# One attention layer with routed experts: slots of two head pairs, r made once, position copies on ScalarE

## The reference, cut to what matters

```
Q, K, V = X @ Wq + bq, X @ Wk, X @ Wv          # 16 heads of 64
R       = X @ Wr + br                          # 16 heads of 10
extra   = einsum('bhtn,ntp->bhtp', R, D)       # D[n, t, p] = b_nd[n, t - p] where 0 <= t - p < 128, else 0
logits  = Q K^T / 8 + bias + extra             # bias = -1e9 outside that window
out     = softmax(logits) V, then @ Wproj + bproj
# experts: each token goes to 2 of 8 (w1, exact gelu, w2), weighted by a softmax over the two
```

## Time and profile before

| what | value |
|---|---|
| median of three runs | 1502.11 us |
| the profiled execution, its own time | 1502.1 us |
| its span | 1500.3 us |
| TensorE matmul busy | 1390.5 us (93%) |
| VectorE busy | 994.2 us (66%) |
| ScalarE busy | 963.8 us (64%) |
| GpSimd busy | 758.2 us (51%) |
| mean granted TensorE clock | 0.967 of full speed |

### The profile page before, as it was taken

How to read it: one execution, slowest core, us unless ns; L and a number is a source line. 1 busy time by engine, 2 the same in 40 slices (tenths; PEclk the granted TensorE clock), 3 DMA queues, 4 the chain that set the end, 5 groups by cost and what they waited for, 6 DMA issues and landing times.

```text
span 1500.3 us, 37780 instructions
## 1 busy us (share of the span) xinstructions
PE 1390.5 (93%) x10823; PEld 1144.7 (76%) x10823; DVE 994.2 (66%) x4355; ACT 963.8 (64%) x2992; POOL 758.2 (51%) x1520
## 2 busy tenths in 40 slices
PE   2572999999999999999999999799999999999997
PEld 1231788888888888878999999688888888888886
DVE  4677677777777777772222221288888888888886
ACT  1121777777777777775454545387777777777775
POOL 1241566676776667660000000167777666777764
PEclk8695999999999999999999999899999999999999
DMA  9775666666666666645666666567676666767662
GB/s 284 269 247 176 188 177 194 183 180 186 187 189 183 185 190 183 183 128 180 210 192 212 200 204 200 150 189 193 184 193 188 180 185 172 194 186 192 188 177 66
DMA packets 441412, 283.00 MB, mean 189 GB/s; under 512 B 18666, under 2 KB 415508, under 8 KB 441236
## 3 DMA queue, kind: packets, MB, share of 16 engines
q1 hardware_dynamic: 433044, 264.12, 61.1%
q0 software_dynamic: 8192, 16.79, 3.9%
HBM read 135.01 MB, written 145.77 MB: 187 GB/s over the span
## 4 chain that ended last, share of the span: by engine, by line
PE 86%; DVE 5%; SPq 3%; DMA 2%; issue 2%; POOL 1%; ACT 1%; DVEq 0%; ACTq 0%; POOLq 0%
PE ps L1420 14%; PE ps L1440 12%; PE ps L1345 9%; PE ps L1309 9%; PE ps L1310 9%; PE ps L1311 9%; PE ps L1450 9%; PE ps L1409 8%; PE ps L1380 4%; PE ps L1327 1%; DMA skew<-gst 1%; SPq L400 1%; DMA wproj<-in_L_attn_Wproj_dram 1%; DMA xn_d<-xn 1%; SPq L453 1%
## 5 line engine op out<-in xcount | busy, mean ns | idle before, releaser
L810 ACT ACTIVATE prob<-logit,low 128x128 f32<-128x128 f32 x1024 | 403.6, 395 | 232.1 <-DVE low L1120 230.0
L1120 DVE CUSTOM_DVE_ANT_0 logit<-ps,extra 128x128 f32<-128x128 f32 x1024 | 256.4, 288 | 190.8 <-PE ps L1420 179.8
L676 POOL TENSOR_SCALAR prob<-prob,inv 128x128 f32<-128x128 f32 x512 | 189.0, 369 | 237.1 <-DVE inv L1106 233.4
L1420 PE MATMUL ps<-qk 64*128 64x256 f32 (+1 forms) x2048 | 237.7, 351 | 2.2 <-DVE low L1120 2.2
L1420 PEld LDWEIGHTS ps<-qk 64*128 64x128 f32 x2048 | 177.4, 187 | 78.7 <-issue 33.7
L1094 DVE TENSOR_TENSOR probT<-ps,keep 128x256 f32<-128x256 f32 x512 | 214.0, 418 | 26.6 <-PE ps L1409 25.7
L1409 PE MATMUL ps<-ident,prob 128*128 128x128 f32 x1024 | 200.5, 279 | 0.4 <-POOL prob L678 0.3
L1440 PE MATMUL ps<-probT,val 128*64 128x256 f32 (+1 forms) x2048 | 194.7, 332 | 5.4 <-DVE probT L1095 5.4
L810 ACT ACTIVATION_READ_ACCUMULATOR prob<-logit,low 128x1 f32 x1024 | 191.1, 187 | 0.0
L651 POOL CAST r_hi<-r_raw 120x512 fp32r<-120x512 f32 x64 | 39.6, 618 | 297.5 <-ACT r_raw L773 297.4
L678 POOL TENSOR_SCALAR prob<-prob,inv 128x128 f32<-128x128 f32 x512 | 186.9, 365 | 0.0
(11 more groups left out here) (179 smaller groups left out, 2792.2 us busy)
## 6 DMA issues: line engine op xcount, KB each, us to landing
skew<-gst SPq DMA_DIRECT2D x384, 256.0 KB
extra<-skew SPq DMA_DIRECT2D x256, 256.0 KB, 3.4
w1b<-w_d SPq DMA_DIRECT2D x39, 514.0 KB, 3.5
w2b<-w_d SPq DMA_DIRECT2D x39, 320.0 KB, 3.3
x_place<-zero SPq DMA_DIRECT2D x39, 256.0 KB, 2.8
placed<-x_place SPq DMA_DIRECT2D x39, 256.0 KB, 3.7
y_place<-yrow SPq DMA_DIRECT2D x39, 256.0 KB, 2.2
w_d<-w1s SPq DMA_DIRECT2D x1, 4112.0 KB, 11.9
```

Of the source, the lines that this page charges most:

```text
L676: nc.gpsimd.tensor_scalar(prob[:, h, 0:P], prob[:, h, 0:P], inv[:, h, 0:1], 1.0, ALU.mult, ALU.mult).then_inc(norm_made, 1)
L810: ins = nc.scalar.activation(prob[:, h % PB, a:b], logit[:, h % LB, a:b], ACT.Exp, scale=-1.0, bias=low[:, h % LB, t:t + 1], accum_out=tot ...
L1120: ins = nc.vector.tensor_tensor_reduce(out=logit[:, h % LB, a:b], in0=ps[:, S_BANK[n], a:b], in1=extra[:, h, a:b], scale=1.0, scalar=BIG, ...
L1420: mm = nc.tensor.matmul(ps[:, S_BANK[n], cols], qk[rows, pair % 2, 0, q], qk[rows, pair % 2, 1, k], start=True, stop=True)
```

## The change

It regroups attention into double slots d = 0 to 3 of two pairs (four heads) and changes four things.

- TensorE makes the logits of both pairs in one go (banks 0 to 3), then the values, and the outputs later in the same double slot, between keys and a position unit. The transposes of a pair (four) come together and use one bank. The units have one bank instead of two.
- r is made once, in one unit of six products with 80 rows, for all 16 heads. GpSimd rounds it to r_hi and subtracts to r_lo; six DMAs of SyncE (`spread_weights`) then put high, high and low part into rT, which is there twice (even and odd sequences).
- All g are copied by ScalarE.
- VectorE takes one reciprocal for four heads, at the head of the next double slot, and masks the transposes of a pair in two instructions instead of four. The row moves of GpSimd have other places, yget has two buffers, and rows are added in four steps.

The table of units and the start:

```diff
-        UNITS = [(0, 0, "v", 0, 0, 0), (0, 1, "g", 3, 0, 0), (1, 0, "r", 0, 0, 1), (1, 1, "g", 3, 1, 0),
...
+        UNITS = [(0, 0, "v", 0, 0, 0), (0, 1, "g", 2, 1, 0), (0, 2, "r", 0, 0, 1), (0, 3, "g", 3, 0, 0),
...
-        START = [("r", 0, 0), ("r", 1, 0)] + [("g", g, t) for g in range(3) for t in range(2)]
+        START = [(kind, k, t) for _, _, kind, k, t, ahead in UNITS if ahead]
```

The order on TensorE:

```diff
+            def sequence(i, start, heads=True, more=True):
+                for d in range(QUADS if heads else LAG):
...
+                    if to_come:
+                        keys(*later)
                     if heads:
-                        units(i, par, j, 0, more)
-                        logits(i, j)
...
+                        units(i, d, 0, more)
+                        logits(i, d)
+                    if here(i, d - 2, heads, start):
+                        values(i, d - 2)
                     if heads:
-                        units(i, par, j, 1, more)
...
+                        units(i, d, 1, more)
+                    if here(i, d - 1, heads, start):
+                        turn_probs(i, 2 * (d - 1))
+                    if to_come:
+                        keys(later[0], later[1] + 1)
+                    if heads:
+                        units(i, d, 2, more)
+                    if here(i, d - 2, heads, start):
+                        outputs(i, d - 2)
+                    if heads:
+                        units(i, d, 3, more)
+                    if here(i, d - 1, heads, start):
+                        turn_probs(i, 2 * (d - 1) + 1)
```

The way of r:

```diff
+            def spread_weights(seq):
+
+                par = seq % 2
+                sp.wait_ge(r_low, seq + 1)
+                for t in range(2):
+                    wait_from(sp, g_made[t], 4 * (seq - 1))
+                for s, part in enumerate((r_hi, r_hi, r_lo)):
+                    for a in range(2):
+                        sp.dma_start(rT[s * PER * NB:(s + 1) * PER * NB, par, :, a, :].bitcast(F32),
+                                     part[a * PER * NB:(a + 1) * PER * NB, :].bitcast(F32).rearrange("p (k q) -> p k q", q=T)
+                                     ).then_inc(r_in[par], 16)
...
-            def round_weights(seq, k):
-
-                wait_apart(pool, r_copied, 2 * seq + (k + 1), const_made)
-                nc.gpsimd.tensor_copy(r_hi[:, k, :], r_raw[:, k, :]).then_inc(r_high, 1)
+            def round_weights(seq):
+
+                pool.wait_ge(r_copied, seq + 1)
+                if seq > 0:
+                    pool.wait_ge(r_in[(seq - 1) % 2], (seq + 1) // 2 * 96)
+                nc.gpsimd.tensor_copy(r_hi[:, :], r_raw[:, :]).then_inc(r_high, 1)
+                pool.wait_ge(r_high, seq + 1)
+                nc.gpsimd.tensor_tensor(r_lo[:, :], r_raw[:, :], r_hi[:, :].bitcast(F32), ALU.subtract).then_inc(r_low, 1)
...
-                nc.vector.scalar_tensor_tensor(out=rT[:, k, :], in0=r_hi[:, k, :].bitcast(F32), scalar=minus_low[0:RS, :],
-                                               in1=r_raw[:, k, :], op0=ALU.mult, op1=ALU.add).then_inc(r_made, 1)
```

The reciprocals and ScalarE's order:

```diff
+            def inverses(i, quad):
+
+                h = 4 * quad % PB
+                dve.wait_ge(prob_made, i * PAIRS + 2 * quad + 2)
+                wait_from(dve, norm_made, 8 * (i * QUADS + quad - 1))
+                nc.vector.reciprocal(inv[:, h:h + 4, :], total[:, h:h + 4, :]).then_inc(inv_made, 1)
...
+                    units(d, 0)
+                    if to_come:
+                        keys(*later)
                     if heads:
...
+                        exponentials(i, 2 * d, 0)
+                    if here(i, d - 2, heads, start):
+                        heads_out(i, d - 2)
+                    units(d, 1)
+                    if heads:
+                        exponentials(i, 2 * d, 1)
+                    units(d, 2)
+                    if to_come:
+                        keys(later[0], later[1] + 1)
+                    units(d, 3)
+                    if heads:
+                        exponentials(i, 2 * d + 1, 0)
+                        exponentials(i, 2 * d + 1, 1)
```

More of the change, by code:

```diff
@@ new lines, in moves_of, with norms @@
+            def moves_of(i, way, d, more):
+                moves = MOVES_FINAL if way is FORTH and not more else MOVES
+                return [n for n, at_d in enumerate(moves) if at_d == d]
+            def norms(i, d, n):
+                pair = 2 * d + n
+                for h in (2 * pair % PB, 2 * pair % PB + 1):
+                    nc.gpsimd.tensor_scalar(prob[:, h, 0:P], prob[:, h, 0:P], inv[:, h, 0:1], 1.0,
+                                            ALU.mult, ALU.mult).then_inc(norm_made, 1)
+                    nc.gpsimd.tensor_scalar(prob[:, h, P:], prob[:, h, P:], inv[:, h, 1:2], 1.0,
+                                            ALU.mult, ALU.mult).then_inc(norm_made, 1)
@@ L703, in _ @@
+                    if d == 0 and heads and more:
+                        round_weights(i + 1)
             FORTH, BACK = "forth", "back"
@@ L709, in _ @@
                 split_q(s0, 0)
-                for k in range(2):
-                    round_weights(s0, k)
+                round_weights(s0)
                 if way is FORTH:
@@ new lines, in exponentials @@
+            def exponentials(i, pair, t):
+                cols = slice(t * P, (t + 1) * P)
+                act.wait_ge(logit0_made if t == 0 else logit_made, i * PAIRS + pair + 1)
+                if t == 0:
+                    wait_from(act, pT_psum, i * PAIRS + pair + 1 - PB // 2)
+                for h in (2 * pair, 2 * pair + 1):
+                    ins = nc.scalar.activation(prob[:, h % PB, cols], logit[:, h % LB, cols], ACT.Exp,
+                                               scale=-1.0, bias=low[:, h % LB, t:t + 1],
+                                               accum_out=total[:, h % PB, t:t + 1])
+                if t == 1:
+                    ins.then_inc(prob_made, 1)
@@ new lines, in heads_out, with units @@
+            def heads_out(i, quad):
+                act.wait_ge(head_psum, i * QUADS + (quad + 1))
+                wait_from(act, out_psum, i * QUADS + quad)
+                nc.scalar.copy(headT[:, :, :].rearrange("p n t -> p (n t)"),
+                               ps[:, HEAD_BANK, :]).then_inc(head_made, 1)
+            def sequence(i, start, heads=True, more=True):
+                def units(d, place):
+                    for n, kind, k, t, ahead in units_at(d, place, more) if heads else []:
+                        unit(len(START) + i * len(UNITS) + n, kind, k, t, i + ahead)
+                for d in range(QUADS if heads else LAG):
+                    to_come = heads and (d + 1 < QUADS or more)
+                    later = (i, 2 * (d + 1)) if d + 1 < QUADS else (i + 1, 0)
+                    units(d, 0)
+                    if to_come:
+                        keys(*later)
+                    if heads:
+                        exponentials(i, 2 * d, 0)
[11 more added lines that the diff above has]
+                        exponentials(i, 2 * d + 1, 1)
@@ L1137, in sequence @@
-                    for n, kind, k, t, ahead in units_at(j, 0, more) if heads else []:
-                        if kind == "r":
-                            weights(i + 1, k)
-                    if j in ADDS and start == HALF and here(i, -1, heads, start) and heads:
-                        add_rows(i - HALF - 1, ADDS.index(j), i - 1)
+                        copy_probs(i, 2 * (d - 1))
+                    if heads:
+                        bias_sums(i, 2 * d + 1)
+                    if here(i, d - 1, heads, start):
+                        copy_probs(i, 2 * (d - 1) + 1)
@@ L1381, in unit, with units @@
+                        mm = product(ps[0:RP, MISC_BANK, k * T:(k + 1) * T], ((wr_hi[:, cols], wr_lo[:, cols]), x))
+                else:
+                    pe.wait_ge(r_in[par], (seq // 2 + 1) * 96)
+                    mm = nc.tensor.matmul(ps[:, MISC_BANK, :], rT[:, par, n // 2, n % 2, tile * P:(tile + 1) * P], basis[:, :],
                                           start=True, stop=True)
                 mm.then_inc(misc_psum, 1)
-            def units(i, par, slot, place, more):
+            def units(i, d, place, more):
@@ L1386, in units @@
                 table = UNITS if more else UNITS_FINAL
[L1387 to L1389 removed]
+                for n, kind, k, t, ahead in units_at(d, place, more):
+                    if n >= 1:
+                        _, _, kind0, k0, t0, ahead0 = table[n - 1]
                         unit_taken(pe, kind0, k0, t0, i + ahead0)
                     else:
[L1392 to L1393 removed]
```

473 lines of the change are left out of this document (212 added, 261 removed), and 6 rows, old and new, of the table UNITS.

## The result

The changed kernel takes 1510.5 us (median of 5 runs, 1505.93 to 1511.93) against 1502.92 us of the kernel before (5 runs beside them, 1501.95 to 1503.66): ratio 1.0044, 95% interval 1.0026 to 1.0061. It is slower by 0.4%, where 1435 was forecast. The profiled execution is the shortest of the five, 1505.93 us with a span of 1503.8.

A forecast was written before the change was run, and what follows sets the result against it. TensorE was taken as the bound. Span 1500.3 - 50 (logits) - 23 (r) + 4.5 (waits) + 1.7 (starts and ends) = 1433.5, plus 1.8 around it: 1435 us; own range 1425 to 1450, 8 in 10 from 1424 to 1464.

The forecast's parts named there:

- What bounds the kernel: In attention TensorE alone has no gap, busy 37.50 of 37.50 us; the other engines' work is hidden.
- Step 1: Two pairs' logits together save one row-shape visit per double slot on TensorE, 0.39 us each: 50 us, bounds 15 and 50.
- Step 2: Making r once drops six TensorE products of 0.118 us per sequence, 0.71 us each: 23 us in all.
- Steps 3 and 4: ScalarE's added copies fit (26.5 of 30.6 us); the one-reciprocal loop fits narrowly, 7.1 to 7.4 in a 7.5 us double slot.
- Rival D: The loop from reciprocal to reciprocal sets the double slot; at 8.4 us the kernel is slower, 1524 us; chance 0.05.
- Step 5: r's six DMAs into rT land between covered and 0.3 us late; steps 3 to 5 wait 4.5 us in all.
- Starts and ends: First start 2.5 us earlier, second 3 later, about 0.6 lost at each end: together +1.7 us, bounds -8 and +10.
- B: r's DMA hop or GpSimd's queue is late by 1 us or more per sequence: 1460, or 1490 at 2 us; chance 0.12.
- A: The array's surcharge belongs to each logits block, not to the change of shape: 1470 us; chance 0.05.
- C: ScalarE's exponentials stand behind a copy waiting for TensorE, stretching each double slot by 0.3 us: 1473 us; chance 0.07.

The follow-up runs named there:

- experiment 2: Experiment 1 with the logits of a double slot's second pair again behind the transposes of the probabilities: 1516.63 us, ratio 1.0087.
- experiment 1: Changed kernel with r's six DMAs into rT only for sequences 0, 1, 16 and 17, so r of the other 28 is left out: 1462.53 us, ratio 0.9737.
- experiment 5: Changed kernel with two axes of rT swapped, so each DMA writes one 2 KB row per partition instead of two of 1 KB: 1508.73 us, ratio 1.0032.
- experiment 6: Experiment 3 with four more DMAs in 16 sequences, of different memories and partition counts, to time their issue: 1475.26 us in one run.
- experiment 7: Experiment 3 with the keys of the first two pairs moved between the start units of both halves: 1461.83 us, ratio 0.9715.
- experiment 8: Experiment 7 with rT laid out in rows of 2 KB as well: 1459.48 us, ratio 0.9706.
- experiment 4: Changed kernel with two more DMAs of r_hi per sequence, into an unread tile, ahead of those of r_lo: 1592.53 us, ratio 1.0622.
- experiment 3: Changed kernel with the four DMAs of r_hi issued without waiting for r_lo and ahead of one skew write: 1458.48 us, ratio 0.9706.
- experiment 9: Experiment 8 with the keys early in the second half's start alone, the first half in its old order: 1450.41 us, ratio 0.9655.

## Why the prediction was wrong

The span was forecast at 1433.5, and is 1503.8: 70.3 us off. By the table, 44.9 of it lie in the steady part (forecast 28 x (-1.56 - 0.71 + 0.15) = -59.4, measured -14.5) and 25.4 in the rest (forecast -7.4, measured +18.0). A steady sequence takes 32.1 us or more, outside the 30.4 to 31.2 beyond which the prediction called itself wrong.

**What bounds the kernel**: right. What was won came from TensorE's distances; VectorE fell from 28.8 to 24.2 us of a window, which gave nothing.

**Step 1, logits together**: right, and its nearer bound. Two blocks take 1.51 us, the outputs 0.84, and experiment 2 prices the visit at 0.435 where 0.39 was taken.

**Step 2, r once**: right, 0.71. Both steps should bring a sequence to 30.63, and it takes 30.83 (experiment 1). I summed the distances from start to start by the kind of product in one sequence of the kernel before and one of the changed kernel, without the wait for rT: r fell by 0.89 us (0.18 of it the gap before two logits blocks), logits by 0.80, outputs by 0.72, keys by 0.17; but the transposes rose from 2.44 to 2.85, and the position products by 0.11. That makes -2.06 for the -2.27 of the forecast, 5.6 us in 28 sequences. The prediction gave the transposes no term. Inside a group they start 0.11 us apart, and what follows a group starts only 0.03 behind its last one. Before there are 16 groups of two in a sequence, 0.14 to 0.20 us each (307.27 to 307.41, 303.19 to 303.39), now 8 of four at 0.36 (449.99 to 450.35), so 8 of the short distances are gone.

**Steps 3 and 4, ScalarE and the reciprocal**: right in that nothing waits in a steady sequence (3.6 us for prob in the whole run). That the loop takes 7.1 to 7.4 in 7.5 was not measured; experiments 5 to 8 have a wait for VectorE that I take for it, 0.6 us a sequence where it comes. Rival D (a loop of 8.4 us) did not come.

**Step 5, r through DMA: this step failed.** The copy, the cast, and the subtraction at 1.29 for 1.3 were right, and SyncE starts 9.7 us into the sequence where 9.4 was said. The term that was mis-sized is "the six DMAs ... 0.36 to 0.46 each": they take 0.82 each with their gaps (4.89 / 6). So the last one is issued 13.9 us into the sequence instead of 11.2 to 11.7, and the product can start 2.5 us later, within the 2.2 to 3.4 that were said for a landing: at 16.4, where it wants rT at 15.1. (From its own terms the recorded landing would be 13.4 to 15.1; it says 13.5 to 15.3.) I had taken the price of an issue from the rows of skew, transfers with DRAM on one side and 128 partitions. A row of the kernel before had the right kind, small and from SBUF to SBUF, and I did not look for it:

```profile
58.99 3.23 SPq L453 DMA_DIRECT2D basis<-brev_hi  x4
```

0.81 us each, for 5 KB over 10 partitions. Experiment 1 shows that the hop is the cause, 4 that an issue counts in full, 3 that the order and the earlier start of the issues remove nearly all of the wait, and 5 and 6 that the issue time goes with the memories and the partitions, and little, if at all, with the packets. The steady part is 44.3 us longer than in experiment 1. Of these 3.2 are the clock, below, and 41.1 the 28 waits, of which 4.2 were forecast. Twice a wait, of 2.1 us each, was followed by half clock, which cost 1.6 each:

```profile
1247.93 0.47 PE L1415 MATMUL ps<-basis,rT 120*128 120x512 f32 x1 [2.11 <-DMA rT<-r_lo]
...
1249.88 0.63 PE L1346 MATMUL ps<-wv_hi,xq_hi 128*128 128x512 f32 x1
1250.31 0.63 PE L1347 MATMUL ps<-wv_lo,xq_hi 128*128 128x512 f32 x1
```

0.43 apart instead of 0.24. So of the 44.9 waits are 36.9, the distances between products 5.6 and the clock 3.2. Against these stand 1.1 of another kind: the last steady sequence of the kernel before took 34.04 us instead of 32.89, which the changed kernel hasn't. 0.3 is not accounted for.

The Trainium skill, page "DMA: Bandwidth & Descriptors", section "Issuing engines are not separate DMA queues", says that the time which the sequencer takes to initiate a DMA is usually small relative to the DMA itself. By that rule six issues cost little beside one landing. Here it does not hold: one issue takes 0.77 to 0.78 us and the six 4.89, and from the last one's end to the product it is 1.7.

**Starts and ends: failed as well, 25.4 us.** "Products at 952.23 become 957, logits ... 970, 3 later": the wait for rT is 9.75 us and ends 10.7 us behind the first product of r where 8.0 was reckoned, and the logits follow r by 25.75, where the earlier trace rows have 18.2 and I reckoned 21. The first 2.7 us are again the issues, 5.4 us for the six. The other 2.1 lie between the first position product and the logits. That takes 15.05 us, as long as in the kernel before (952.23 to 967.20), where I had 13: the five position products of the single bank take as long, 7.1 us, as the six did on two banks (952.23 to 959.29), and the keys of a third pair stand ahead of the logits. The products, and a window (columns as in the earlier trace rows):

```profile
954.42 0.77 PE L1415 MATMUL ps<-basis,rT 120*128 120x512 f32 x1 [9.75 <-DMA rT<-r_lo]
955.86 0.79 PE L1415 MATMUL ps<-basis,rT 120*128 120x512 f32 x1 [0.68 <-ACT gst L814]
957.33 0.79 PE L1415 MATMUL ps<-basis,rT 120*128 120x512 f32 x1 [0.68 <-ACT gst L814]
958.89 0.79 PE L1415 MATMUL ps<-basis,rT 120*128 120x512 f32 x1 [0.77 <-ACT gst L814]
961.53 0.80 PE L1415 MATMUL ps<-basis,rT 120*128 120x512 f32 x1 [1.85 <-ACT gst L814]
...
969.47 2.93 PE L1459 MATMUL ps<-qk 64*128 64x256 f32 x16
```
```profile
948.40:972.20 23.80, 12.46 (x42) 8.60 (x42) 0.82 (x5) 5.64 (x10) 0.72 (x1) 0.50 0.49 143
```

Each product waits until ScalarE has emptied the bank of the one before, 1.44 to 1.56 us from start to start, though the next product can follow at 0.60 where nothing is waited for (961.53 to 962.13). The last waits longer, 1.85 us, since ScalarE's copy before it waited 2.06 us for a skew write. TensorE goes to half clock during the long wait and stays there for 23.8 us; in the kernel before it was 13.5 (954.8 to 968.3). So the logits of two pairs take 2.87 us (969.47 to 972.34) instead of 1.51. The first sequence of each half then repeats it with longer waits for rT, 3.3 and 2.5 us, each followed by half clock again (sequence 16 takes 34.3 us, where the kernel before has 28.1 and experiment 9, with a wait of 0.5, 30.8). Experiment 3 takes 7.6 of the 18.0 us away, and experiment 9 all but 0.4.

**The rivals.** B came true, with its releaser as named, and from the point it named, a landing after 16.0. At the usual wait of 1.27 us its formula gives 1435 - 4.5 + 38 = 1469; the 37 us from there to the profiled 1506 are the starts (25.4), the distances (5.6), the clock (3.2) and the sequences that waited longer. D, the only rival that forecast a slower kernel, did not come; the changed kernel is slower by B and the starts together. B's chance, 0.12, was too small, and "all pieces measured" was the wrong argument against it: one piece was measured on another kind of transfer, and six in a row multiply its error. A fell by experiment 2, C did not show.

## What to carry to other kernels

Price a DMA's issue by a row of the same kind (which memories, how many partitions), and multiply it by the number in a row: a chain of small SBUF to SBUF copies costs its issues first and one landing after. Send each part as soon as it stands: not holding r_hi back for r_lo and for one skew write costs nothing and was worth 52 us here. And where a term is multiplied by 30, cover of a few tenths is no cover: find the slack of each link before the sum is made.

## What the hardware showed that was not expected

- SyncE needs 0.77 to 0.79 us to issue a DMA of 80 KB from SBUF to SBUF over 40 partitions, 0.71 to 0.72 for rT with rows of 2 KB (and 0.79 for another tile with such rows), 0.54 for 128 KB over 128 partitions, 0.50 to DRAM and 0.33 from DRAM. A DMA of 5 KB over 10 partitions took 0.81.
- In the steady part of the changed kernel half clock followed waits of 2.05 and 2.11 us and not one of 2.00, and in the first half of experiment 4 it did not follow most waits of 2.9 us; the length of one wait does not tell it. In the window shown there the mean clock of the next 3.6 us was 0.57.
- One more visit of TensorE to the split by rows costs 0.435 us (experiment 2), as much as four of its 128-column products.
- The same order of work ran at two steady paces, 30.8 and 31.4 us a sequence, the slower with a wait of 0.5 us for VectorE. The order of the first start moved it from one to the other (experiments 8 and 9), but kernels with the old order show the slower pace too (5 and 6).
